# One reordered first iteration: the fourth token tile fetched from ScalarE's queue, a convolution ahead of the token products, and the out-projection splits moved

## What is computed

```python
proj = input_states @ in_proj_w.T            # gate | x, B, C | dt
xBC = silu(conv_4_taps(xBC) + conv_b)
dt = softplus(dt + dt_bias); dA = dt * A     # A = -exp(A_log)
cum = cumsum(dA)                             # within a chunk
Ldec = exp(cum_i - cum_j), lower triangle
y = (C B^T * Ldec * dt) @ x + state part + D * x
g = y * silu(gate)
g = g * rsqrt(mean(g*g) + EPS) * norm_w      # by group
return g @ out_w.T
```

## Time and profile before

| | us |
|---|---|
| median of 3 runs | 2824.02 |
| lowest and highest run | 2819.71, 2824.45 |
| profiled execution, its own time | 2827.02 |
| its span in the profile | 2825.2 |
| PE busy in it | 2793.4 |
| VectorE, ScalarE, GpSimd busy | 2016.1, 1464.0, 1315.3 |

### The profile page before, as it was taken

How to read it: one execution, slowest core, us unless ns; L and a number is a source line. 1 busy time by engine, 2 the same in 40 slices (tenths; PEclk the granted TensorE clock), 3 DMA queues, 4 the chain that set the end, 5 groups by cost and what they waited for, 6 DMA issues and landing times.

```text
span 2825.2 us, 56341 instructions
## 1 busy us (share of the span) xinstructions
PE 2793.4 (99%) x22190; PEld 2267.1 (80%) x22190; DVE 2016.1 (71%) x3212; ACT 1464.0 (52%) x2206; POOL 1315.3 (47%) x842
## 2 busy tenths in 40 slices
PE   7999999999999999999999999999999999999998
PEld 5888888778788888887888888888888888878886
DVE  7777768887667667677676766677766666666767
ACT  5666666655455545455355454454544445454545
POOL 4767767775343433443334443434434334443334
PEclk9999999999999999999999999999999999999999
DMA  7888777878565565565665565555655656555530
GB/s 246 277 302 297 267 272 258 283 258 294 176 195 184 183 196 170 193 201 176 205 198 182 190 200 169 187 184 187 208 182 190 198 172 207 184 183 187 187 131 31
DMA packets 179508, 578.39 MB, mean 205 GB/s; under 512 B 25264, under 2 KB 31920, under 8 KB 171184
## 3 DMA queue, kind: packets, MB, share of 16 engines
q1 hardware_dynamic: 179248, 574.79, 61.8%
HBM read 460.42 MB, written 114.29 MB: 203 GB/s over the span
## 4 chain that ended last, share of the span: by engine, by line
PE 92%; DVE 5%; ACT 1%; issue 1%; DMA 0%; POOL 0%; SPq 0%; DVEq 0%; ACTq 0%; POOLq 0%
PE p_in L485 54%; PE p_out L485 24%; PE p_y L485 8%; PE p_in L586 4%; DVE cv L1483 1%; PE p_y L724 1%; DVE o_ring L1422 1%; PE p_y L829 0%; DVE t_y L1532 0%; DVE mx L1673 0%; DVE decay L1515 0%; DVE g_f L1544 0%; DVE sc L1660 0%; DVE cum L1444 0%; ACT L975 0%
## 5 line engine op out<-in xcount | busy, mean ns | idle before, releaser
L485 PE MATMUL p_in<-xnb,w_ring 128*128 128x512 f32 x6852 | 1675.8, 397 | 4.5 <-DVE cv L1483 2.0
L485 PEld LDWEIGHTS p_in<-xnb,w_ring 128*128 128x128 f32 x6852 | 1262.8, 189 | 266.5 <-issue 5.7
L1483 DVE SCALAR_TENSOR_TENSOR cv<-p_in,cpar,cv 128x504 f32<-128x504 f32 x954 | 699.9, 734 | 450.3 <-ACT cv L975 426.5
L1938 POOL TENSOR_TENSOR g_lo<-g_f,g_hi 128x512 fp32r<-128x512 f32 x256 | 336.6, 1316 | 1179.2 <-ACT g_hi L975 1179.2
L485 PE MATMUL p_out<-o_ring,g_hi 128*128 128x512 f32 x2048 | 639.3, 393 | 0.5 <-POOL g_lo L1938 0.5
L975 ACT ACTIVATE cv<-p_in,cpar 128x512 f32<-128x512 f32 x318 | 246.7, 776 | 620.4 <-PE p_in L485 584.1
L485 PEld LDWEIGHTS p_out<-o_ring,g_hi 128*128 128x128 f32 x2048 | 380.0, 188 | 78.4 <-issue 0.7
L485 PE MATMUL p_out<-o_ring,g_lo 128*128 128x512 f32 x1024 | 399.9, 390 | 0.0
L1520 DVE TENSOR_TENSOR x_tok<-p_in,dts 128x512 f32<-128x512 f32 x256 | 176.6, 690 | 265.8 <-PE p_in L586 264.4
L975 ACT ACTIVATE x_t<-cv 128x512 f32<-128x512 f32 x256 | 160.8, 628 | 308.2 <-DVE t_y L1532 287.6
L1949 POOL TENSOR_TENSOR ss<-ss,g_sq 128x512 f32<-128x512 f32 x190 | 310.5, 1634 | 7.5
(11 more groups left out here) (275 smaller groups left out, 2232.4 us busy)
## 6 DMA issues: line engine op xcount, KB each, us to landing
w_ring<-ws_scr SPq DMA_DIRECT2D x432, 512.0 KB, 3.7
o_ring<-ows_scr SPq DMA_DIRECT2D x192, 512.0 KB, 4.7
ws_scr<-w_ring SPq DMA_DIRECT2D x144, 512.0 KB, 6.0
decay<-cum_scr SPq DMA_DIRECT2D x126, 512.0 KB, 6.7
raw_w<-wt SPq DMA_DIRECT2D x144, 256.0 KB, 5.3
ows_scr<-o_ring SPq DMA_DIRECT2D x64, 512.0 KB, 6.2
raw_o<-owt SPq DMA_DIRECT2D x64, 256.5 KB, 5.6
xt<-x SPq DMA_DIRECT2D x12, 256.0 KB, 8.4
```

Source lines behind the costliest of these rows:

```text
L485: return nc.tensor.matmul(o, lhsT=l, rhs=r, start=first, stop=last)
L1483: ins = V.scalar_tensor_tensor(acc[:, :, t:SEQ], src[:, :, 0:SEQ - t], cpar[:, 5 * m + 3 - t:5 * m + 4 - t], acc[:, :, t:SEQ], ALU.mult, A ...
L1938: T(g_lo[:, c % 2, :], g_f[:, c % 2, :], g_hi[:, c % 2, :].bitcast(F32), ALU.subtract).then_inc(glo_done, 1)
```

## The change

All edits are in iteration 0 or ahead of it. The fourth token tile is fetched from ScalarE's queue as its first instruction, in place of SyncE's fifth. The low part of the step weights `wd` is subtracted by VectorE, ahead of `lows`, in place of GpSimd. GpSimd waits ahead of `w_low(0, 3)` until VectorE has done the first step of softplus. `split_o(0, 0)` and `o_low(0, 0)` move to the front; `o_low(0, 1)` moves from after `clamped_half(1)` to the end of k = 3. `tap0(4)`, `conv(4)` and `gate(2)` move ahead of the first half of the exponential. Units 8 and 9 get other banks, and unit 8 moves ahead of `heads(0)`, unit 9 ahead of `to_tokens(2)`. `late(0)` (the moments of the next token tile) and its `normal` move up, `conv(5)` moves down behind them. GpSimd does `w_low(0, 9)` ahead of the two halves.

```diff
-        FIRST_STEPS = 19
+        FIRST_SUM, FIRST_STEPS = 5, 19
+        FIRST_BANKS = {2: 0, 3: 1, 4: 2, 5: 3, 7: 1, 8: 3}
...
-            if first(n) and (2 <= k < 6 or k == 7):
-                return p_out[1 if k == 7 else k - 2][:, :]
-            return p_in[k % 2][:, :]
+            if first(n) and k in FIRST_BANKS:
+                return p_out[FIRST_BANKS[k]][:, :]
+            return p_in[0 if first(n) and k == 9 else k % 2][:, :]
... (SyncE)
-            load_x(3)
... (PE)
-            unread(4, TB)
+            unread(5, TB)
...
-                elif first(n) and k == 7:
-                    pe.wait_ge(gate_done, 1)
+                elif first(n) and k in (7, 8):
+                    pe.wait_ge(gate_done, k - 6)
+                elif first(n) and k == 9:
+                    pe.wait_ge(conv_done, 5)
+                elif first(n) and k == 10:
+                    pe.wait_ge(gate_done, 4)
...
-                        pe.wait_ge(*((gate_done, 3) if first(n) else (acc_done, n)))
+                        pe.wait_ge(*((conv_done, 6) if first(n) else (acc_done, n)))
+                    if c == 0 and first(n):
+                        pe.wait_ge(gate_done, 3)
...
                     to_tokens(1, n)
+                    unit(8, tb, g, n)
...
-                    if begun or k > 2:
+                    if begun or k > 3:
                         unit(3 + 2 * k, tb, g, n)
-                    else:
-                        unit(8, tb, g, n)
+                    elif k == 2:
+                        unit(9, tb, g, n)
... (ScalarE)
+            act.dma_start(acb[:, 0, 3, :], x[3 * P:4 * P, :]).then_inc(x0_in[3], 16)
...
                 split_w(0, k)
+            split_o(0, 0)
             act.wait_ge(wdl_done, 1)
...
                     tap0(2, n)
+                    split_w(0, 8, 3)
                     silu(1, n)
                     tap0(3, n)
-                    split_w(0, 8, 3)
+                    split_w(0, 9, 4)
                     silu(2, n)
+                    tap0(4, n)
                     silu(3, n)
+                    gate(2, n)
                     exp_half(0)
+                    tap0(5, n)
... (VectorE)
+            dve.wait_ge(wdh_done, 1)
+            V.tensor_tensor(wd[:, 1, :, :].rearrange("p k c -> p (k c)"), d_s[:, :],
+                            wd[:, 0, :, :].rearrange("p k c -> p (k c)").bitcast(F32), ALU.subtract).then_inc(wdl_done, 1)
             for q in range(QT):
                 lows(q)
...
             skips(0, 0)
+            o_low(0, 0)
             softplus(0, (*range(16), 17, 18))
...
                     conv(3, n)
+                    conv(4, n)
                 products(n)
...
                     decayed_half(0)
+                    late(0, tb, g)
...
-                    if k == 3 and not begun:
-                        decayed_half(1)
...
                     x_tokens(k, n)
+                    if k == 3 and not begun:
+                        decayed_half(1)
...
                     if k == 2 and not begun:
-                        late(0, tb, g)
-                        refill_o(0)
+                        normal(QT, xt[:, :], xt[:, :], QT)
                         conv(5, n)
                         clamped_half(1)
-                        refill_o(1)
...
+                    if k == 3 and not begun:
+                        refill_o(1)
                     if k == 3:
                         refill_o(k)
... (GpSimd)
-            pool.wait_ge(wdh_done, 1)
-            T(wd[:, 1, :, :].rearrange("p k c -> p (k c)"), d_s[:, :],
-              wd[:, 0, :, :].rearrange("p k c -> p (k c)").bitcast(F32), ALU.subtract).then_inc(wdl_done, 1)
...
             for k in range(RING_W):
+                if k == 3:
+                    pool.wait_ge(dve_own, FIRST_SUM)
                 w_low(0, k)
```

More of the change, by code:

```diff
@@ L580, in to_tokens @@
             def to_tokens(c, n):
-                if first(n) and c == 1:
-                    pe.wait_ge(xtok_done, 1)
+                if first(n) and c in (1, 3):
+                    pe.wait_ge(xtok_done, c)
                 pe.wait_ge(silu_done, CONVS * n + 3 + c)
@@ L1161, in body @@
                         silu_table()
-                    if k == 2 and not begun:
-                        split_w(0, 9, 4)
-                        refill_o(0)
                     if k == 3 and tb == 0:
@@ L1169, in body @@
                         silu(2 + k, n)
-                        gate(k, n)
+                        if begun or k > 2:
+                            gate(k, n)
                         g_high(k - 2, n)
@@ L1187, in body @@
                     if k == 2 and not begun:
-                        tap0(5, n)
                         refill(1)
@@ L1434, in softplus @@
                         link(V.tensor_scalar(cum[:, :], d_e[:, :], 2.0, None, ALU.add))
+                        assert b or own[0] == FIRST_SUM
                     if part in (1, 2):
@@ L1805, in body @@
                     decayed_half(0)
+                    late(0, tb, g)
                 dve.wait_ge(dpar_done, n + 1)
                 for k in range(1 if begun else 2, CPG):
-                    if k == 3 and not begun:
-                        normal(QT, xt[:, :], xt[:, :], QT)
-                    if begun or k != 3:
+                    if begun or k > 3:
                         conv(2 + k, n)
@@ L2020, in body @@
                         w_low(0, 8)
+                        w_low(0, 9)
                         for half in range(2):
                             differences_half(half)
-                        w_low(0, 9)
                     if k == 1 and begun and coming(tb, g) is not None:
@@ L2037, in body @@
                     if k % 2 == 0:
-                        g_low(k - 2, n)
                         if k == 2 and not begun:
                             deviation(coming(tb, g))
+                        g_low(k - 2, n)
                         if k == 2 and tb == 0:
```

2 lines of the change are left out of this document (1 added, 1 removed).

## The result

| | before | after |
|---|---|---|
| median of 11 runs each, us | 2824.02 | 2831.34 |
| lowest and highest run | 2819.71, 2829.31 | 2829.69, 2835.92 |
| after over before, with 95% interval | | 1.0027 (1.0018 to 1.0036) |
| profiled execution: own time, span | 2827.02, 2825.2 | 2835.92, 2833.9 |

The change makes the kernel 0.27% slower, 7.3 us in the median. The forecast was 2828.0 with a range up to 2834.0: the sign and the mechanism came as written, the size was 3.3 us short. The profiled execution of the changed kernel is the slowest of its eleven, 4.6 us above their median; that of the kernel before is 3.0 above its own. So their rows are compared in stretches and not by their totals.

What follows compares the result with a forecast made beforehand. PE was taken as the bound, busy 2793.4 of 2825.2 us. To to_tokens(4) -1.2 us, plus 5.1 for half clock, gave +3.9: 2828.0 against the median of 2824.02, range 2821.5 to 2834.0.

Steps and rivals of the forecast that it cites:

- the sign and the mechanism: First iteration: slower by 3.9 us; o_low(0,1) beside GpSimd's differences delays SyncE's raw_o fetch, PE idles some 8 us before to_tokens(4).
- a sum at full clock: Steps up to the end of decayed_half(1), priced without slow clock: 62.1 against 67.8 before, a win of 5.7 us.
- Two collisions: VectorE beside GpSimd's differences: o_low(0,1), ending 4.35 us after decayed_half(1); later decayed(1) or o_low, +3 to +5 us, chance 0.23.

Runs made afterwards that it cites:

- run 4: The changed kernel with the fourth token tile fetched again by SyncE, fifth in its queue: 2830.89 us, ratio 1.0028 to the kernel before.

## What to carry over

When an instruction moves, follow what its semaphore releases: here a 0.75 us subtraction sat in front of a DMA queue, and one place in the order was worth 4.8 us of the median. A gain on a path that ends in a wait should be priced with the clock that the gap will cost, and a baseline that already ran in part at half clock must not be compared with a sum at full clock. Where executions of one kernel differ in clock, the distance of a profiled execution from the median belongs to that execution (3.0 us before, 4.6 changed, -0.2 in run 4) and can't be handed on to another kernel. Two collisions that each shift by the same lateness add up.
